# Another order of the last two batches' feed-forward work in a transformer layer's ending

## The reference

```python
x = x + attn(layernorm(x), wq, wk, wv, wo)
x = x + ffn(layernorm(x), weight, bias)
```

```python
x_scale = jnp.maximum(jnp.max(jnp.abs(x), axis=2, keepdims=True) / 127.0, 1e-12)
x_q = jnp.clip(jnp.round(x / x_scale), -128, 127)
y = einsum('bnd,od->bno', x_q, w_q) * x_scale * w_scale + bias
```

## Time and profile before

| | before |
|---|---|
| median of 3 runs | 637.77 us (637.02 to 639.27) |
| the profiled execution | 637.02 us |
| its span | 635.2 us |
| TensorE busy | 600.9 us, 95% |
| VectorE busy | 543.0 us, 85% |
| ScalarE busy | 401.2 us, 63% |
| GpSimd busy | 307.8 us, 48% |
| mean granted TensorE clock | 0.991 |

### The profile page before, as it was taken

The page is one execution under the profiler, slowest core; times in us unless marked ns, Lnnn a source line. Parts: engine busy times, 40 slices in busy tenths (PEclk is TensorE's granted clock), DMA queues, the critical chain, the costliest instruction groups (busy, mean ns, idle before and its releaser), DMA issues.

```text
span 635.2 us, 18267 instructions
## 1 busy us (share of the span) xinstructions
PE 600.9 (95%) x7586; PEld 530.4 (83%) x7586; DVE 543.0 (85%) x1081; ACT 401.2 (63%) x633; POOL 307.8 (48%) x302
## 2 busy tenths in 40 slices
PE   4778999999999999999999999999999999999983
PEld 3556988889898888989898888989898888989872
DVE  4777689989888998979898998989898898989885
ACT  4766776566666666667666666666666666665740
POOL 1132435455554646455564646456554745535440
PEclk9989999999999999999999999999999999999997
DMA  8921311202021221202121120302121120202100
GB/s 287 355 62 45 92 44 31 72 13 88 20 73 47 53 66 28 92 5 82 34 67 54 43 77 17 101 3 84 34 58 62 39 81 13 89 19 66 53 19 33
DMA packets 35698, 41.33 MB, mean 65 GB/s; under 512 B 5792, under 2 KB 26272, under 8 KB 35616
## 3 DMA queue, kind: packets, MB, share of 16 engines
q1 hardware_dynamic: 35472, 40.03, 21.0%
q10 hardware_dynamic: 144, 0.13, 0.1%
HBM read 10.26 MB, written 4.19 MB: 23 GB/s over the span
## 4 chain that ended last, share of the span: by engine, by line
PE 87%; DVE 6%; ACT 3%; issue 1%; DMA 1%; POOL 1%; SPq 0%; POOLq 0%; ACTq 0%
PE ps L533 26%; PE ps L409 25%; PE ps L436 7%; PE ps L385 6%; PE ps L376 6%; PE ps L492 5%; PE ps L515 4%; PE ps L516 4%; ACT mag L681 1%; PE ps L366 1%; PE ps L560 1%; DMA small<-in_L_attn_wv 1%; PE ps L548 1%; DVE Qs L872 1%; DVE WoT L985 0%
## 5 line engine op out<-in xcount | busy, mean ns | idle before, releaser
L409 PE MATMUL ps<-xT,WqT 128*128 128x256 f16 x1536 | 181.1, 275 | 1.1 <-DVE WqT L985 0.5
L533 PE MATMUL ps<-WoT,pool 128*128 128x256 f16 x1536 | 178.0, 273 | 0.2 <-DVE pool L896 0.2
L409 PEld LDWEIGHTS ps<-xT,WqT 128*128 128x128 f16 x1536 | 148.0, 98 | 19.1 <-issue 1.5
L533 PEld LDWEIGHTS ps<-WoT,pool 128*128 128x128 f16 x1536 | 147.5, 98 | 16.4 <-DVE pool L896 0.3
L1174 POOL TENSOR_TENSOR small<-E,rr 128x576 f32<-128x576 f32 x63 | 72.6, 1152 | 104.2 <-DVE rr L891 104.2
L752 ACT ACTIVATE pool<-ps 128x512 f16<-128x512 f32 x128 | 69.5, 594 | 83.8 <-PE ps L516 83.7
L1180 POOL TENSOR_TENSOR PP<-small,PP 128x576 f16<-128x576 f32 x63 | 80.9, 1284 | 65.4 <-ACT PP L745 65.4
L712 ACT ACTIVATE Qs<-ps 128x576 f16<-128x576 f32 x128 | 82.6, 646 | 46.7 <-PE ps L409 46.7
L872 DVE TENSOR_TENSOR Qs<-ps,Qs 128x576 f16<-128x576 f32 x128 | 92.6, 724 | 5.1 <-ACT Qs L712 4.9
L1166 POOL TENSOR_TENSOR Sm<-Sm,mx 128x576 f32<-128x576 f32 x64 | 73.7, 1152 | 42.1 <-DVE mx L882 40.8
L896 DVE SCALAR_TENSOR_TENSOR pool<-ps,pool 128x512 f16<-128x512 f32 x128 | 81.8, 680 | 1.9 <-ACT pool L752 1.9
(11 more groups left out here) (110 smaller groups left out, 882.4 us busy)
## 6 DMA issues: line engine op xcount, KB each, us to landing
VW<-Vn SPq DMA_DIRECT2D x48, 120.0 KB
big<-Vn SPq DMA_DIRECT2D x48, 120.0 KB
X<-in_L_attn_x SPq DMA_DIRECT2D x16, 256.0 KB, 7.3
out<-pool SPq DMA_DIRECT2D x15, 256.0 KB, 2.3
VW<-Vn SPq DMA_DIRECT2D x48, 60.0 KB
big<-Vn SPq DMA_DIRECT2D x48, 60.0 KB
big<-in_L_attn_wq SPq DMA_DIRECT2D x4, 512.0 KB, 8.1
pool<-in_L_attn_wo SPq DMA_DIRECT2D x4, 512.0 KB, 9.0
```

Source lines behind the costliest of these rows:

```text
L409: a = pe.matmul(banks[BANK_Q[f]][:, j * 256:j * 256 + 256], WqT[:, k, wl, h * 128:h * 128 + 128], xT[:, b % 2, k, xl, :], start=(n == 1), ...
L533: a = pe.matmul(banks[BANK_OUT][:, t * 256:t * 256 + 256], OT[:, p, ol, h, t * 128:t * 128 + 128], WoT[:, 4 * g + h, wl, :], start=first, ...
```

## The change

On SyncE and ScalarE, the stores of the last two batches: before, batch 14 went out as one store of 256 KB on SyncE's queue once both halves were done, the first half of batch 15 on SyncE's queue and the second on ScalarE's. Now there are four stores of a half each, all on SyncE's queue, each as soon as its half is done.

On TensorE, `ffn_t(14)` stands ahead of `out_proj(63)` and not behind it.

On VectorE, three calls move: `ffn_residual(14)` from behind `o_low(60)` to behind `s_max(63)`; `ffn_quant(14)` from behind `o_low(63)` to ahead of it; `with_bias(14)` from behind `ffn_quant(14)` to just ahead of `ffn_out(14)`.

```diff
@@ sync
-            sp.wait_ge(f_z, 2)
-            sp.dma_start(out_v[B - 2], yo[:, B % 2]).then_inc(out[B % 2], 16)
-            sp.wait_ge(f_z, 3)
-            sp.dma_start(out_v[B - 1][:, 0, :], yo[:, (B - 1) % 2, 0, :]).then_inc(out[(B - 1) % 2], 16)
-            sp.wait_ge(out[0], 16 * (B // 2))
+            for b in (B - 2, B - 1):
+                for t in range(2):
+                    sp.wait_ge(f_z, 2 * (b - B + 2) + t + 1)
+                    sp.dma_start(out_v[b][:, t, :], yo[:, b % 2, t, :]).then_inc(out[b % 2], 16)
+            sp.wait_ge(out[0], 16 * (B // 2 + 1))
             sp.wait_ge(out[1], 16 * (B // 2 + 1))
@@ tensor
             out_proj(u)
+            ffn_t(B - 2)
             out_proj(u + 1)
-            ffn_t(B - 2)
             ffn_mm(B - 2)
@@ scalar
             ffn_t_evac(B - 1)
-            act.wait_ge(f_z, 4)
-            act.dma_start(out_v[B - 1][:, 1, :], yo[:, (B - 1) % 2, 1, :]).then_inc(out[(B - 1) % 2], 16)
@@ vector
             o_low(u - 2, 1)
-            ffn_residual(B - 2)
             q_low(u + 1, 0)
             q_low(u + 1, 1)
             probs(u)
             s_max(u + 1)
+            ffn_residual(B - 2)
             ffn_stats(B - 2)
...
             ffn_norm(B - 2)
+            ffn_quant(B - 2)
             o_low(u + 1, 0)
             o_low(u + 1, 1)
-            ffn_quant(B - 2)
-            with_bias(B - 2)
             ffn_residual(B - 1)
             ffn_stats(B - 1)
             with_bias(B - 1)
             ffn_norm(B - 1)
             ffn_quant(B - 1)
+            with_bias(B - 2)
             ffn_out(B - 2)
             ffn_out(B - 1)
```

## The result

The changed kernel is slower. Over 16 runs each its median is 642.70 us (639.35 to 644.12), that of the kernel before 638.75 (636.79 to 641.57). The ratio is 1.0054, 95% interval 1.0039 to 1.0069: +3.4 us, between 2.5 and 4.4 (the two medians are 3.95 apart, which lies within this). I had forecast +1.9 us, and 639.7 with a range of 638.5 to 641.4; the median lies outside it. One microsecond of that miss is the base: the three runs that I had showed 637.77, sixteen show 638.75. The rest is in the main a misjudged rival.

What follows compares the result with a forecast made beforehand. It took TensorE, busy 95% of the span, as the bound, with every edit in the ending. The terms 1.66 + 0.22 + 0 + 0 gave +1.9 us on the 637.77 median, so 639.7 us, range 638.5 to 641.4.

Steps and rivals of the forecast that it cites:

- Edit 1: ffn_residual(14) behind s_max(63) on VectorE: out_proj(60) starts 2.46 us later, of which 1.66 us reach the transposes of unit 63.
- Edit 2: ffn_t(14) ahead of out_proj(63) on TensorE: its four transposes add 0.22 us to the path.
- Edit 3: ffn_quant(14) ahead of o_low(63), with_bias(14) later on VectorE: both hidden, o_low(63) with 0.2 to 0.4 us spare, cost zero.
- rival (d): Cover fails on VectorE: with_bias(14) shows or o_low(63) comes late, up to 0.68 us more, 640.4; chance 0.10.
- Edit 4: Stores of batches 14 and 15 in halves on SyncE's queue: taken as zero, bounds 0.55 us gain, 0.5 loss.
- Rival (b): The end, with its changed stores, gives back up to 0.55 us: +1.35, 639.1 us; chance 0.12.
- rival (a): TensorE's clock falls in the new hole before out_proj(60), costing 1.7 us more, 641.4 us; chance 0.10.

Runs made afterwards that it cites:

- e3: Changed kernel plus 21 matmuls that nobody reads between scores(63) and out_proj(60) on TensorE; 639.82 us against 639.44, ratio 1.0013.
- a1: Second trace of the changed kernel as it is, one execution; 35.5 us from the start of scores(63) to the end.
- a2: Third trace of the changed kernel as it is, one execution; 35.7 us from the start of scores(63) to the end.
- b1: Second trace of the kernel before as it is, one execution; 33.5 us from the start of scores(63) to the end.
- v3: v2 plus 22 unread matmuls in TensorE's wait at 39 us and 14 before the first PV; 638.55 us against 638.81, ratio 0.9994.
- e1: Changed kernel with ffn_residual(14) back at its old place, all other moves kept; 637.85 us against 639.44, ratio 0.9994.
- e4: Changed kernel with ffn_residual(14) between probs(62) and s_max(63) on VectorE; 638.60 us against 639.44, ratio 1.0000.
- b2: Third trace of the kernel before as it is, one execution; 33.5 us from the start of scores(63) to the end.
- v2: v1 plus 12 unread matmuls before PV of unit 62 and 7 before PV of unit 63; 638.14 us against 638.81, ratio 0.9989.
- v1: Kernel before plus unread matmuls released by batch 15's steps, and with_bias(15) behind ffn_quant(15); 637.79 us against 639.31, ratio 0.9979.

## Why the prediction was wrong, point by point

**Edit 1, the stall: right.** Forecast 2.46 us at out_proj(60), measured 2.54 (3.34 - 0.80). PV of unit 62 was released by ScalarE's copy of PT, as said; in the chain of waits after:

```profile
617.15 1.03 ACT PT L727
618.18 0.05 issue
618.22 0.23 PE ps L514
```

Of the stall 1.66 us were to reach the transposes of unit 63. e3, the trace with the stall and without a fall, has them 616.30 - 603.65 = 12.65 us after scores(63), before 10.95 (611.56 + 2.62 - 603.23 by the earlier trace rows): 1.70.

**Edit 2: right.** 0.22 forecast, 0.22 measured. Together with edit 1, residual(15) was to be 1.88 later; in e3 it is 21.01 - 19.10 = 1.91.

**Edit 3: one half right.** o_low(63) stayed hidden: in the trace after it began at 625.31 and ended at 626.59, and out_proj(63) started at 627.31 behind ffn_t(14) with no wait. In e3, without a fall, o_low(63) ended at 621.13 and out_proj(63) started at 621.84. That is 0.7 us to spare in both, more than the 0.2 to 0.4 forecast. The statistics of batch 14 stayed hidden as well: probs(63) starts 4.61 us after scores(63), before 4.62. with_bias(14) was to cost nothing, with 0.72 us of idle time to hold 0.68. It costs 0.83 from start to start and shows 0.1 to 0.2: a small piece of rival (d). I had taken the instruction's own length and left out that the next one waits for its end.

**Edit 4: right.** 2.2 us from VectorE's end to the end of the span, before and after. Rival (b) did not come.

**The sum and the rival.** The four edits give 1.9 + 0.2 = 2.1 us when the clock stays, which is e3: 34.05 - 31.97. What failed is the weight of rival (a), to which I gave 0.10: the sum put the fall of the clock at nothing. Its price was right: 35.75 - 34.05 = 1.7 us in the profiled execution, 1.4 and 1.6 in a1 and a2, forecast 1.7. Its mechanism was right. Its chance was not: it came in four traces of four. The same error hides in the other half of the sum, since I took the ending of the kernel before as free of falls, and it has one of 1.6 us in three traces of five. The step that failed is "Against: from 51 to 55 us TensorE worked 1.00 of 4.00 us and kept 1.00". That was one execution. In other executions the clock did fall just behind that same stretch; b1's windows:

```profile
50.00:55.50 5.50, 2.20 (x51) 1.90 (x50) 4.12 (x6) 2.98 (x5) 2.32 (x2) 1.00 0.24 82
55.80:59.00 3.20, 3.20 (x17) 2.28 (x16) 1.70 (x3) 1.55 (x3) 0.00 (x0) 0.50 0.02 5
```

The code up to there is the same in all traces but v3's. In nine of those thirteen the clock fell behind that stretch, and they take 549.9 us from the first PV to scores(63); in four (before, a1, e1, e4) it held, and they take 548.2. So one trace in which the clock held was no evidence that it holds. The Trainium skill (TensorE: Matmul & The Clock Gate, Part 1 on the HAM clock gate), which I had cited, says that the monitor is not aligned with the kernel. I concluded from it that some executions would be struck, and not that the row I held against it was one draw from the same lot. That much of it the traces bear out: with the same code the clock fell in the ending in b1 and b2 and not in the first trace.

A second, smaller error was the base. Three runs of a kernel whose runs scatter by 5 us do not fix its median to a microsecond.

## What to carry to other kernels

Moving an instruction later on one engine is free only if nobody waits for what it signals: look up every semaphore that it raises, also for waits that the diff does not show. A new idle stretch on TensorE has two prices, the wait and a fall of the clock behind it, and the second can be as large as the first; one trace cannot tell how often it comes, so price it in, or fill the stretch with matmuls that nobody reads. That was clear of noise in e3; v2 and v3, which do so in the kernel before, were not. Compare endings from a common point next to the change, not by spans, when the beginning of the program scatters by more than the effect.

## What the runs showed of the hardware

TensorE's clock fell around stretches that were by no means all idle. In the changed kernel TensorE had worked 0.96 us in scores(63), rested 2.39, and in three of four traces was at work again for 0.9 to 1.0 us when it fell; in a1 it fell while TensorE still rested. In the kernel before it fell within 0.4 us after the end of an idle time of 1.61 us (b1, b2 and v1), or not at all (before and e1).

A fall cost 1.4 to 1.7 us in the hole, 1.6 in front of out_proj(61) and 1.67 behind the first PV near 57 us. Behind residual(15), where VectorE is last, the full clock made TensorE's last eight matmuls 0.6 us shorter and the kernel only 0.2 (v1).

The falls are one reason why executions of the same code differ here. The start of scores(63) lay anywhere from 603.2 to 607.9 us. Of this the fall behind the first PV makes 1.67, in two clear groups. The rest lies ahead of the first PV, which starts at 53.8 to 58.0 us, and does not follow the number of falls: e1, whose clock was at 0.50 for some 14 us before that, has it at 55.49, the first trace of before, with 3.4 us at 0.50, at 55.04. Over the 92 executions of the kernel before for which a mean granted clock is on record, the six with 0.991 took 635.9 to 637.6 us and the eight with 0.977 took 640.9 to 642.0; in between the order is loose. What makes the rest of the scatter was not tested; v3 was the attempt on the falls near the beginning, and filled only one of the stretches long enough.
